# First masked attention: the mask's matmuls open every other step and close the rest, and two queues bring the operand stacks

## The chip, the cores and the metric

The kernel is one program on 1 core of a Trainium2 chip. The metric is the device time in microseconds of one execution. Every duration below comes from one profiled execution, or from the repeated timings, which are named as such.

## What is computed

Four examples of 512 rows and 256 features pass through a masked cross attention, a routed mixture of eight experts, a second cross attention with memory rows and a quantized feed-forward stack. Only the first attention is touched:

```python
def L0_xattn(q, kv, mask):              # q = layernorm(x), kv = ctx, 16 heads of 16
    qh, kh, vh = heads(q @ Wq.T + bq), heads(kv @ Wk.T + bk), heads(kv @ Wv.T + bv)
    attn = einsum('bhqd,bhkd->bhqk', qh, kh) * 16 ** -0.5
    attn = softmax(where(mask, -inf, attn), axis=-1)     # one mask for all heads
    return concat_heads(einsum('bhqk,bhkd->bhqd', attn, vh)) @ Wo.T + bo

x = x + L0_xattn(layernorm(x), ctx, mask)      # the part that the change touches
x = x + L0_ffn(layernorm(x))                   # 8 experts, one per row, gated
x = x + L1_xattn(layernorm(x), ctx)            # 16 heads of 64, 128 memory rows
x = x + L1_ffn(layernorm(x))                   # three residual quantized blocks
return x                                       # x: 4 x 512 x 256, float32
```

## The kernel before

`attention0` runs first, over the four examples. One pass over an example is a **turn**. The 16 heads go in four **groups** of four, g = 0 to 3, and each group in eight **steps**, j = 0 to 7. A step treats one tile of 128 keys (kt = j // 2) for one pair of heads (slot = j % 2), against all 512 queries. A prologue before the first turn does the same preparation that a turn does for the next example.

TensorE (PE) is the engine that does most of the work. Its order within a step is the table `STEPS` (lines 144 to 153), whose words stand for:

- `score` (L667): scores of one head, 64 rows by 128 columns of the array, 512 queries streamed. The two heads of a pair lie in the two halves of the rows and go together. `q_stack` and `k_stack` hold each head's 16 features three times, as rounded and remaining parts (hi, hi, lo against hi, lo, hi), with the negated row maximum in the last row.
- `bias` (L677): four 64 by 64 bf16 matmuls that add the mask to both heads' scores in PSUM. The last one tells ScalarE, through `s_full`, that the step's scores are whole.
- `maximum`, `early` (L639): scores in the other orientation, of the next group (`early`: the one after it), whose row maxima VectorE takes. Two such matmuls lie in the two halves of the rows. A group has 16: four early, twelve in steps 0 to 5.
- `times_v` (L687): exponentials times values, 128 rows by 32 columns a head, eight records for four heads. It follows the exponential of the step before its own, which ScalarE reports in `exp_done`.
- `query`, `key` (L619): projections for the next half of the heads, in g = 0 and 2. `turn` (L646) transposes the group's maxima; `sums` (L651) spreads the previous group's reciprocal sums; `rows` (L605) transposes normalized rows.

The matmuls of `maximum`, `turn`, `sums`, `query` and `key` share three PSUM banks, `p_m`, in rotation. `Banks.free` makes PE wait until the bank taken three fills earlier has been read. The scores have two buffers, `p_s`; a step waits in `score` until the exponential two steps back is done.

VectorE (DVE) follows PE's fills in the same order: `maximum` (L468) adds the mask, reduces and frees the bank. It also splits projections (`split`, L460: lo = full - hi), normalizes (L485) and reads out the turn's last matmuls. ScalarE (ACT) writes `full` and `hi` (L353), takes the exponentials (L362) and copies outputs (L366).

The **stacks** are brought by DMA (`bring`, L252) from `hi` and `lo`, 64 KB a DMA, six for one stack and group. All are issued from SyncE's queue (SP), in this order for each half: queries' stack of the half's first group, keys' stack of that group, the maxima of group g + 1 (`bring_maxima`, L270), then both stacks of the half's last group. The reader of the first group's stacks is the `early` of step 6 in g = 0 and g = 2. GpSimd (POOL) takes reciprocal square roots (L320) and adds the output bias (L326), once an example.

## Time and profile before

| | |
|---|---|
| median of 3 runs | 1547.67 us (1545.13 to 1551.35) |
| the profiled execution, its own time | 1540.11 us |
| its span, first to last instruction | 1538.3 us |
| mean granted TensorE clock over the span | 0.936 of full speed |
| first attention: prologue, then four turns | 0 to 48 us, 48 to about 394 us |

The profile has a page (busy shares, 40 slices, queues, chains, groups of instructions) and views of the trace: a timeline of instructions in order of time, a list of waits, and busy times of chosen stretches. A record of a matmul begins with its weight load when that load is not hidden, and ends after the pipeline is through, so records of neighbouring matmuls overlap. What counts is the distance between starts. A releaser in brackets is what ended the idle time before an instruction. `PEld` is the weight load, and `SPq` an issue on SyncE's queue.

### The profile page before, as it was taken

The page shows a single profiled execution, that of the slowest core. Times are in us where ns is not written, and L with a number is a line of the kernel's source. Part 1 is how long each engine was busy: PE and PEld are TensorE (multiplying, and loading weights), DVE is VectorE, ACT ScalarE, POOL GpSimd, SP SyncE. Part 2 cuts the span into 40 slices and gives each one's busy share as a digit, 9 for nine tenths or more (in the row PEclk, how much of TensorE's full clock was granted, in tenths as well). Part 3 has the DMA queues.
Part 4 walks back from the last instruction along what each step waited for, and adds up shares of the span by engine and source line. Part 5 has one row for each costly group of instructions (what it writes and reads, how often), then busy time and mean ns, then how long its engine had stood idle before and what let it go on. Part 6 is the DMA issues. An engine that isn't in the chain of part 4 may idle for free. (4 is left out here: it accounts for less than half of the span.)

```text
span 1538.3 us, 19109 instructions
## 1 busy us (share of the span) xinstructions
PE 1377.1 (90%) x6106; PEld 733.4 (48%) x6106; DVE 876.9 (57%) x1738; ACT 477.4 (31%) x678; POOL 450.0 (29%) x262
## 2 busy tenths in 40 slices
PE   4889889989554999966999999999999999998997
PEld 2324333343352776642444455444544455435886
DVE  5656666555341222236576655756576665786677
ACT  1343434435111222211333332333233332341221
POOL 2000000000123000031454534445354543473443
PEclk8799999899756999986999999999999999999998
DMA  6410112101238988844556552655256552610001
GB/s 181 162 43 8 51 40 55 42 22 23 68 122 252 319 309 312 313 117 107 88 77 96 83 83 42 97 82 83 41 82 96 82 82 43 113 63 21 0 1 55
DMA packets 71273, 152.13 MB, mean 99 GB/s; under 512 B 17888, under 2 KB 28640, under 8 KB 64544
## 3 DMA queue, kind: packets, MB, share of 16 engines
q1 hardware_dynamic: 65392, 143.82, 41.2%
q0 software_dynamic: 2640, 7.21, 1.4%
q8 instruction: 37, 0.61, 0.2%
q10 hardware_dynamic: 3168, 0.20, 0.1%
q14 instruction: 36, 0.29, 0.1%
HBM read 75.49 MB, written 10.22 MB: 56 GB/s over the span
## 5 line engine op out<-in xcount | busy, mean ns | idle before, releaser
L1198 POOL TENSOR_TENSOR a_probs<-a_probs 128x1024 f32<-128x1024 f32 x128 | 304.9, 2382 | 379.2 <-PE a_p_mo L1868 378.7
L1270 ACT ACTIVATE a_probs<-a_p_s 128x1024 f32<-128x1024 f32 x160 | 163.8, 1024 | 340.7 <-PE a_p_s L1854 340.7
L468 DVE CUSTOM_DVE_ANT_0 a_scratch<-a_p_m,a_bias_q 128x512 bf16<-128x512 f32 x256 | 163.3, 687 | 97.3 <-PE a_p_m L639 97.2
L1502 DVE TENSOR_REDUCE a_max_ctx<-a_p_mo 128x1 f32<-128x512 f32 x256 | 161.5, 684 | 75.1 <-PE a_p_mo L1825 75.1
L362 ACT ACTIVATE a_probs<-a_p_s 128x1024 f32<-128x1024 f32 x128 | 129.1, 1024 | 113.6 <-PE a_p_s L677 112.3
L1868 PE MATMUL a_p_mo<-a_probs,a_v 128*64 128x512 f32 x512 | 139.0, 621 | 0.0
L1853 PE MATMUL a_p_s<-a_q_hh,a_k_hl 128*128 128x512 f32 x256 | 128.5, 502 | 0.0
L639 PE MATMUL a_p_m<-a_k_stack,a_q_stack 63*128 63x512 f32 x256 | 88.9, 543 | 24.3 <-DMA a_k_stack<-a_hi 22.1
L1525 DVE RECIPROCAL a_recip<-a_p_mo 128x512 f32<-128x512 f32 x32 | 107.4, 3355 | 5.0 <-PE a_p_mo L1877 4.9
L1854 PE MATMUL a_p_s<-a_q_lm,a_k_h 65*128 65x512 f32 x256 | 101.9, 398 | 0.0
L1246 ACT ACTIVATE a_o_norm<-a_p_mo,a_b 128x128 f32<-128x128 f32 x184 | 49.9, 382 | 151.9 <-PE a_p_mo L1730 151.9
L1720 PE MATMUL a_p_s<-a_w,a_o_raw 128*128 128x512 f32 x184 | 84.7, 604 | 0.0
L1740 PE MATMUL a_p_mo<-a_w,a_o_norm 128*128 128x256 f32 x368 | 83.3, 379 | 0.1
L1853 PEld LDWEIGHTS a_p_s<-a_q_hh,a_k_hl 128*128 128x128 f32 x256 | 49.1, 192 | 63.3 <-issue 37.2
L1825 PE MATMUL a_p_mo<-a_k_hl,a_q_hh 64*128 64x512 f32 x256 | 67.6, 484 | 11.6 <-DMA a_q_lm<-a_lo 7.5
L687 PE MATMUL a_p_o<-a_probs,a_v 128*32 128x512 f32 x512 | 71.7, 633 | 6.8 <-ACT a_probs L362 4.8
L1419 DVE COPY a_o_norm<-a_p_s 128x512 f32<-128x512 f32 x46 | 31.8, 692 | 74.7 <-PE a_p_s L1720 74.7
L1493 DVE SCALAR_TENSOR_TENSOR a_lo<-a_p_mo,a_bqk,a_hi 128x512 fp32r<-128x512 f32 x58 | 43.2, 745 | 54.6 <-ACT a_hi L1260 52.1
L1740 PEld LDWEIGHTS a_p_mo<-a_w,a_o_norm 128*128 128x128 f32 x368 | 68.2, 190 | 9.1 <-issue 0.8
L1260 ACT ACTIVATE a_hi<-a_p_mo,a_bqk 128x512 fp32r<-128x512 f32 x58 | 39.9, 687 | 100.5 <-PE a_p_mo L1799 100.5
L320 POOL TENSOR_TENSOR a_rstd<-a_rstd,a_minus_half 128x4 f32<-128x4 f32 x4 | 4.1, 1024 | 225.9 <-DVE a_rstd L428 225.9
L1799 PE MATMUL a_p_mo<-a_xn_t,a_space 128*128 128x512 f32 x116 | 62.6, 666 | 6.9 <-DVE a_recip L1525 6.5
(221 smaller groups left out, 2110.3 us busy)
## 6 DMA issues: line engine op xcount, KB each, us to landing
a_w<-in_L_w SPq DMA_DIRECT2D x46, 1024.0 KB, 6.6
a_q_hh<-a_hi SPq DMA_DIRECT2D x64, 256.0 KB, 5.1
a_k_hl<-a_hi SPq DMA_DIRECT2D x64, 128.0 KB, 6.1
a_k_hl<-a_lo SPq DMA_DIRECT2D x64, 128.0 KB, 6.5
a_k_h<-a_hi SPq DMA_DIRECT2D x32, 256.0 KB, 7.8
a_q_lm<-a_lo SPq DMA_DIRECT2D x32, 256.0 KB, 6.8
a_ctx_t<-in_ctx_t SPq DMA_DIRECT2D x8, 512.0 KB, 4.3
a_q_stack<-a_hi SPq DMA_DIRECT2D x64, 64.0 KB, 2.2
```

What stands on the lines that cost most here:

```text
L362: act.activation(probs[:, j % 4, :, :], p_s[:, j % 2, :, :], ACT.Exp).then_inc(exp_done.sem, 1)
L468: dve.tensor_tensor_reduce(scratch[:, fill.n % M_BANKS, :], m, bias_q[:, t, :], 1.0, -3.0e38, ALU.add, ALU.max, mx[:, g % 2, at:at + 1]).t ...
L639: done(pe.matmul(m, q_stack[rows, pair, P * t:P * (t + 1)], k_stack[rows, pair, :], start=True, stop=True))
L1198: pool.tensor_tensor(probs[:, kt], probs[:, kt - 1], probs[:, kt], ALU.add)\
L1270: act.activation(probs[:, kt, :, :], p_s[:, (KT1 * p + kt) % 2, :, :], ACT.Exp).then_inc(exp_done.sem, 1)
L1502: dve.tensor_reduce(max_ctx[:, NT * head + t:NT * head + t + 1], m, AX, ALU.max)\
L1525: dve.reciprocal(recip[:], m).then_inc(m_free.sem, 1)
L1720: mm = pe.matmul(p_h[:, HALVES * (n % 2) + half, :], rows_t[:, n % 2, k, :], w1[:, n % RING, k, S * half:S * (half + 1)], start=(k == 0), ...
L1740: mm = pe.matmul(p_y, hidden[:, n % 2, d, :], w2[:, n % RING, d, :], start=(d == 0), stop=(d == FC - 1))
L1853: pe.matmul(p_s[:, n % 2, i, :], first, q_hh[:, s, :], start=True, stop=False)
L1854: mm = pe.matmul(p_s[:, n % 2, i, :], second, q_lm[:, s, :], start=False, stop=True)
L1868: mm = pe.matmul(p_o[DK * i:DK * (i + 1), :], vh, probs[:, kt, i, :], start=(kt == 0), stop=(kt == KT1 - 1))
```

## The change

Even steps 2, 4 and 6 keep scores first and have the mask's matmuls end the accumulation; odd steps 1, 3 and 5 and step 0 begin with the mask's, and the second score ends it and signals `s_full`. In steps 2 and 4 the two maxima now stand between scores and mask, and in step 7 the scores and two early maxima do. `sums` moves from the head of step 7 to step 6, between `turn` and the first two early maxima. The keys' stacks are issued from GpSimd's queue, both groups of a half in one go, with semaphores of their own. In the prologue, VectorE's three small operations for `nan_row` come after the early maxima, and the DMA that makes `bias_s` follows `bias_k` directly.

```diff
-        SCORE2 = ("score", "score", "bias")
-        STEPS = (("query", *SCORE2, *MAX2, "times_v"),
-                 ("key", *SCORE2, *MAX2),
-                 (*SCORE2, *MAX2, "times_v"),
-                 (*SCORE2, *MAX2),
-                 (*SCORE2, *MAX2, "times_v"),
-                 (*SCORE2, *MAX2),
-                 (*SCORE2, "times_v", "turn", *EARLY2),
-                 ("sums", *SCORE2, *EARLY2, "rows"))
+        SCORE2 = ("score", "score")
+
+        STEPS = (("query", "bias", *SCORE2, *MAX2, "times_v"),
+                 ("key", "bias", *SCORE2, *MAX2),
+                 (*SCORE2, *MAX2, "bias", "times_v"),
+                 ("bias", *SCORE2, *MAX2),
+                 (*SCORE2, *MAX2, "bias", "times_v"),
+                 ("bias", *SCORE2, *MAX2),
+                 (*SCORE2, "bias", "times_v", "turn", "sums", *EARLY2),
+                 (*SCORE2, *EARLY2, "bias", "rows"))
...
-        stacked = [Count(sem("stacked_first"), 16 * 24), Count(sem("stacked_last"), 16 * 24)]
+        stacked = [Count(sem(f"{stack}_{group}"), 16 * 12) for stack in ("queries", "keys") for group in ("first", "last")]
...
+        def bring(queue, half, group, n):
...
+                    queue.dma_start(stack[HALF * side + DH0 * k:HALF * side + DH0 * (k + 1), at:at + G0 // 2, :].bitcast(F32),
+                                    part[src:src + SLOT, n, :].bitcast(F32)).then_inc(stacked[2 * n + group].sem, 16)
...
             def stack(b, half):
 
-                for n in range(2):
-                    split_ready.wait(sp, b, 2 * half + n + 1)
-                    bring(half, 0, n)
+                split_ready.wait(sp, b, 2 * half + 1)
+                bring(sp, half, 0, 0)
 
             def stack_last(half):
 
-                for n in range(2):
-                    bring(half, 1, n)
+                bring(sp, half, 1, 0)
...
+            def stack_keys(b, half):
+                split_ready.wait_apart(pool, b, 2 * half + 2, consts, 2)
+                for group in range(2):
+                    bring(pool, half, group, 1)
+
             invert_deviation(-1)
+            stack_keys(-1, 2)
             pool.wait_ge(loaded, 16 * 5)
             bias(-1)
             with pool.Fori(0, B - 1) as b:
+                stack_keys(b, 1)
                 invert_deviation(b)
                 bias(b)
+                stack_keys(b, 2)
+            stack_keys(B - 1, 1)
...
-            dve.tensor_scalar(bias_k[:], mask_in[:, 1, :, :], -MASKED, None, ALU.mult)
+            dve.tensor_scalar(bias_k[:], mask_in[:, 1, :, :], -MASKED, None, ALU.mult).then_inc(prep, 1)
             dve.wait_ge(prep, 2)
-            dve.tensor_reduce(least_masked[:], bias_q[:], AX, ALU.max).then_inc(prep, 1)
...
             for i in range(N_MAX):
                 maximum(-1, fill, NG0, i)
             turn_maxima(-1, fill, NG0)
             for i in range(N_EARLY):
                 maximum(-1, fill, NG0 + 1, i)
+            dve.tensor_reduce(least_masked[:], bias_q[:], AX, ALU.max).then_inc(prep, 1)
...
+            def free_scores(b, g, j):
+
+                n = PARTS * g + j
+                if n >= 2:
+                    exp_done.wait_apart(pe, b, n - 1, consts, 2)
...
-                pe.matmul(p_s[:, slot, i, :], k_stack[rows, pair, P * kt:P * (kt + 1)], q_stack[rows, pair, :],
-                          start=True, stop=False)
+                mm = pe.matmul(p_s[:, slot, i, :], k_stack[rows, pair, P * kt:P * (kt + 1)], q_stack[rows, pair, :],
+                               start=not masked, stop=masked)
+                if masked and i == 1:
+                    mm.then_inc(s_full.sem, 1)
...
-                        mm = pe.matmul(p_s[keys, slot, i, :], ident_b[rows, rows], bias[rows, kt, :], start=False, stop=True)
-                mm.then_inc(s_full.sem, 1)
+                        mm = pe.matmul(p_s[keys, slot, i, :], ident_b[rows, rows], bias[rows, kt, :], start=not scored, stop=scored)
+                if scored:
+                    mm.then_inc(s_full.sem, 1)
```

On PE, steps 4 and 5 of group 1 in a turn. `a_p_s<-a_q_stack` is the pair of scores, `a_p_s<-a_bias` the mask, `a_p_m<-a_k_stack` a maximum, `a_p_o` the values product. Before:

```order
L667 MATMUL a_p_s<-a_q_stack,a_k_stack 128x512 x2
L677 MATMUL a_p_s<-a_bias_k,a_ident_b 64x512 x2
L677 MATMUL a_p_s<-a_bias_s,a_ident_b 64x512 x2
L62 REGISTER_ALU
L639 MATMUL a_p_m<-a_k_stack,a_q_stack 128x512
L62 REGISTER_ALU
L639 MATMUL a_p_m<-a_k_stack,a_q_stack 128x512
L62 REGISTER_ALU
L687 MATMUL a_p_o<-a_probs,a_v 32x512 x4
L667 MATMUL a_p_s<-a_q_stack,a_k_stack 128x512 x2
L677 MATMUL a_p_s<-a_bias_k,a_ident_b 64x512 x2
L677 MATMUL a_p_s<-a_bias_s,a_ident_b 64x512 x2
```

Now:

```order
L679 MATMUL a_p_s<-a_q_stack,a_k_stack 128x512 x2
L62 REGISTER_ALU
L648 MATMUL a_p_m<-a_k_stack,a_q_stack 128x512
L62 REGISTER_ALU
L648 MATMUL a_p_m<-a_k_stack,a_q_stack 128x512
L691 MATMUL a_p_s<-a_bias_k,a_ident_b 64x512 x2
L691 MATMUL a_p_s<-a_bias_s,a_ident_b 64x512 x2
L62 REGISTER_ALU
L702 MATMUL a_p_o<-a_probs,a_v 32x512 x4
L691 MATMUL a_p_s<-a_bias_k,a_ident_b 64x512 x2
L691 MATMUL a_p_s<-a_bias_s,a_ident_b 64x512 x2
L679 MATMUL a_p_s<-a_q_stack,a_k_stack 128x512 x2
```

The two maxima stand ahead of the mask now, and the next step's mask follows the values product. Scores and maxima of an odd step and the even step after it are now neighbours.

On PE, steps 6 and 7 of group 1; `a_ident,a_mx` is `turn`, `a_recip_rows,a_spread` is `sums`. Before:

```order
L687 MATMUL a_p_o<-a_probs,a_v 32x512 x4
L62 REGISTER_ALU x2
L646 MATMUL a_p_m<-a_ident,a_mx 16x128
L62 REGISTER_ALU
L639 MATMUL a_p_m<-a_k_stack,a_q_stack 128x512 x2
L62 ISA
L651 MATMUL a_p_m<-a_recip_rows,a_spread 128x512
L667 MATMUL a_p_s<-a_q_stack,a_k_stack 128x512 x2
L677 MATMUL a_p_s<-a_bias_k,a_ident_b 64x512 x2
L677 MATMUL a_p_s<-a_bias_s,a_ident_b 64x512 x2
L62 REGISTER_ALU
L639 MATMUL a_p_m<-a_k_stack,a_q_stack 128x512
```

Now:

```order
L702 MATMUL a_p_o<-a_probs,a_v 32x512 x4
L62 REGISTER_ALU x2
L655 MATMUL a_p_m<-a_ident,a_mx 16x128
L62 REGISTER_ALU
L62 ISA
L660 MATMUL a_p_m<-a_recip_rows,a_spread 128x512
L648 MATMUL a_p_m<-a_k_stack,a_q_stack 128x512 x2
L679 MATMUL a_p_s<-a_q_stack,a_k_stack 128x512 x2
L648 MATMUL a_p_m<-a_k_stack,a_q_stack 128x512
L62 REGISTER_ALU
L648 MATMUL a_p_m<-a_k_stack,a_q_stack 128x512
L691 MATMUL a_p_s<-a_bias_k,a_ident_b 64x512 x2
```

`sums` stands ahead of the first two early maxima, and step 7's scores have early maxima, then the mask, behind them.

On POOL, from the head of the loop over examples. Before:

```order
L332 ISA
L320 TENSOR_TENSOR a_rstd<-a_rstd,a_minus_half 128x4
L62 REGISTER_ALU
L326 ISA
L326 TENSOR_TENSOR x_all<-x_all,a_bo 128x1024
L332 REGISTER_ALU
L332 COMPARE_AND_BRANCH
```

Now:

```order
L337 ISA
L237 DMA a_k_stack<-a_hi 16x2x512 x2
L237 DMA a_k_stack<-a_lo 16x2x512 x2
L237 DMA a_k_stack<-a_hi 16x2x512 x4
L237 DMA a_k_stack<-a_lo 16x2x512 x2
L237 DMA a_k_stack<-a_hi 16x2x512 x2
L62 ISA
L319 TENSOR_TENSOR a_rstd<-a_rstd,a_minus_half 128x4
L62 REGISTER_ALU
L325 ISA
L325 TENSOR_TENSOR x_all<-x_all,a_bo 128x1024
L68 REGISTER_ALU
```

Twelve issues precede the reciprocal square root, and twelve more follow the bias. SP keeps the queries' issues and the maxima between them.

## Rows read from the trace of the kernel before

**Rows 1.** Busy times of one turn: us, then PE, PEld, DVE, ACT, POOL busy, granted clock, DMA.

```profile
141.38:233.05 91.67, 82.55 (x469) 33.23 (x468) 57.95 (x167) 39.22 (x44) 3.39 (x2) 0.98 0.17 41
```

**Rows 2.** Waits of PE, 48 to 400 us: who, on whom, us, times, longest.

```profile
PE a_p_m L639 <- DMA a_k_stack<-a_hi: 15.6, 7, 2.6
```

**Rows 3.** Timeline (start us, us), 204.8 to 208.5 us, steps 1 and 2 of group 3.

```profile
204.85 0.50 PE L667 MATMUL a_p_s<-a_q_stack,a_k_stack 64*128 64x512 f32 x2
...
205.28 0.11 PEld L677 LDWEIGHTS a_p_s<-a_bias_k,a_ident_b 64*64 64x64 bf16 x2 [0.25 <-issue]
...
205.62 0.50 PE L639 MATMUL a_p_m<-a_k_stack,a_q_stack 63*128 63x512 f32 x2
...
205.95 0.40 PE L667 MATMUL a_p_s<-a_q_stack,a_k_stack 64*128 64x512 f32 x2
...
206.28 0.11 PEld L677 LDWEIGHTS a_p_s<-a_bias_k,a_ident_b 64*64 64x64 bf16 x2 [0.37 <-issue]
...
207.01 0.18 PEld L639 LDWEIGHTS a_p_m<-a_k_stack,a_q_stack 63*128 63x128 f32 x1 [0.21 <-DVE a_mx L468]
...
207.44 1.07 PE L687 MATMUL a_p_o<-a_probs,a_v 128*32 128x512 f32 x8
...
208.44 0.49 PE L667 MATMUL a_p_s<-a_q_stack,a_k_stack 64*128 64x512 f32 x2
```

**Rows 4.** Timeline, 144 to 165 us, group 0 of example 1: keys' stacks and their reader.

```profile
144.83 1.98 PE L619 MATMUL a_p_m<-a_ctx_t,a_wk 128*128 128x512 f32 x4 [0.36 <-ACT a_hi L353]
...
151.21 0.69 DVE L460 TENSOR_TENSOR a_lo<-a_full,a_hi 128x512 fp32r<-128x512 f32 x1
...
153.98 1.19 SPq L252 DMA_DIRECT2D a_k_stack<-a_hi  x2
...
156.96 0.28 PE L646 MATMUL a_p_m<-a_ident,a_mx 128*16 128x128 f32 x1
...
159.40 0.50 PE L639 MATMUL a_p_m<-a_k_stack,a_q_stack 63*128 63x512 f32 x2 [2.16 <-DMA a_k_stack<-a_hi]
```

**Rows 5.** Timeline, 466 to 500 us, DMAs that GpSimd issues.

```profile
467.18 0.96 POOL L1173 DMA_INDIRECT x_slots<-a_probs,a_slot  x1 [0.30 <-issue]
...
496.68 0.60 POOL L1179 DMA_DIRECT2D y_slots<-a_yb  x1 [15.19 <-DVE a_yb L1426]
```

**Rows 6.** DMA issues: KB each, median us from issue to landing.

```profile
a_k_stack<-a_hi SPq DMA_DIRECT2D x64, 64.0 KB, 2.2
...
y_slots<-a_yb POOLq DMA_DIRECT2D x23, 128.0 KB, 2.6
```

**Rows 7.** Busy times, from a first early maximum to the second values product behind it.

```profile
251.05:258.68 7.63, 6.96 (x43) 2.85 (x43) 6.81 (x24) 4.20 (x5) 1.02 (x1) 1.00 0.44 104
291.13:302.85 11.72, 11.72 (x44) 3.73 (x45) 5.80 (x16) 4.36 (x5) 0.00 (x0) 0.56 0.28 68
```

**Rows 8.** Timeline, 20 to 50 us, the prologue.

```profile
21.58 0.69 DVE L460 TENSOR_TENSOR a_lo<-a_full,a_hi 128x512 fp32r<-128x512 f32 x1 [0.94 <-ACT a_hi L353]
...
26.25 2.28 DVE L561 TENSOR_REDUCE a_least_masked<-a_bias_q 128x4 f32<-128x2048 bf16 x1
...
30.19 1.19 PE L639 MATMUL a_p_m<-a_k_stack,a_q_stack 63*128 63x512 f32 x3 [6.50 <-DMA a_k_stack<-a_hi]
...
49.78 0.69 DVE L468 CUSTOM_DVE_ANT_0 a_scratch<-a_p_m,a_bias_q 128x512 bf16<-128x512 f32 x1 [4.86 <-PE a_p_m L639]
```

**Rows 9.** Timeline, 214.6 to 221 us, the end of group 3, example 1.

```profile
215.00 0.28 PE L646 MATMUL a_p_m<-a_ident,a_mx 128*16 128x128 f32 x1
...
215.81 1.12 PE L651 MATMUL a_p_m<-a_recip_rows,a_spread 128*128 128x512 f32 x2
...
217.08 0.68 DVE L485 TENSOR_TENSOR a_o_norm<-a_o_norm,a_p_m 128x512 f32<-128x512 f32 x1
217.29 0.11 PEld L677 LDWEIGHTS a_p_s<-a_bias_k,a_ident_b 64*64 64x64 bf16 x2 [0.24 <-issue]
...
218.83 1.06 PE L687 MATMUL a_p_o<-a_probs,a_v 128*32 128x512 f32 x8 [0.70 <-ACT a_probs L362]
```

More of the change, by code:

```diff
@@ L226, in bank @@
                 return p_m[:, (BEFORE + self.n - 1) % M_BANKS, :]
+        halves = ((q_stack, (hi, hi, lo)), (k_stack, (hi, lo, hi)))
+        def bring(queue, half, group, n):
+            stack, parts = halves[n]
+            at = PAIR0 // 2 * (half % 2) + G0 // 2 * group
+            for k, part in enumerate(parts):
+                for side in range(2):
+                    src = HALF * group + SLOT * side
+                    queue.dma_start(stack[HALF * side + DH0 * k:HALF * side + DH0 * (k + 1), at:at + G0 // 2, :].bitcast(F32),
+                                    part[src:src + SLOT, n, :].bitcast(F32)).then_inc(stacked[2 * n + group].sem, 16)
         @block.sync
@@ L349, in project @@
                 for count in stacked:
-                    count.wait(act, b, 16 * 12 * half)
+                    count.wait(act, b, 16 * 6 * half)
                 at = half % 2
@@ L458, in split @@
                     for count in stacked:
-                        count.wait(dve, b, 16 * 12 * half)
+                        count.wait(dve, b, 16 * 6 * half)
                 dve.tensor_tensor(lo[:, n, :], full[:, n, :], hi[:, n, :].bitcast(F32),
@@ L464, in maximum @@
                 m = fill.bank()
-                m_full.wait_apart(dve, b, fill.n, prep, 5)
+                m_full.wait_apart(dve, b, fill.n, prep, 3)
                 side, t, pair = maximum_of(i)
@@ L637, in maximum @@
                 if i == 0:
-                    stacked[g % 2].wait(pe, b, 16 * 12 * (g // 2 + 1))
+                    for n in range(2):
+                        stacked[2 * n + g % 2].wait(pe, b, 16 * 6 * (g // 2 + 1))
                 done(pe.matmul(m, q_stack[rows, pair, P * t:P * (t + 1)], k_stack[rows, pair, :],
@@ L698, in turn @@
                     for j in range(PARTS):
-                        head = 0
+                        head, masked = 0, False
                         for what in steps(g, j, ahead):
+                            if what in ("score", "bias") and not head and not masked:
+                                free_scores(b, g, j)
                             if what in ("query", "key"):
```

31 lines of the change are left out of this document (10 added, 21 removed).

## Prediction

> **What bounds the kernel now.** I read four views in this order. The busy times of one turn come first [rows 1]: in 91.67 us PE is busy 82.55, DVE 57.95, ACT 39.22 and POOL 3.39. PE bounds this stage, so what a part is worth is read from its path. The list of waits shows where PE stands still [rows 2]: 15.6 us in seven waits of up to 2.6 us for a keys' stack. The timeline of two ordinary steps shows what PE's order costs [rows 3]. The timeline of group 0 shows how the seven waits arise [rows 4]. The prologue [rows 8] and the end of a turn [rows 9] complete the picture. Behind 394 us no code that runs is changed, and I cost that part at nothing.
>
> The steps in [rows 3] are to be read by their starts. The scores start at 204.85, their mask at 205.28, the maxima at 205.62, the next scores at 205.95, their mask at 206.28, the fourth maximum at 207.01, the values product at 207.44, and the following step at 208.44. A pair of steps thus takes 3.59 us. Scores behind another tile shape need 0.43 to the mask, and scores behind maxima, which have their shape, need 0.33: the weight load is hidden, worth 0.10. The first maximum to the fourth takes 1.39 us. There are three banks, so the fourth waits until DVE has read the first. This small loop, not the matmuls, sets part of each pair.
>
> **The change, part by part. Pairs of steps (1,2) and (3,4).** After the change a pair is mask (0.34), scores (0.33), first maximum, fourth maximum, mask, values product. First to fourth is again DVE's round trip, 1.39 less 0.10, because the first maximum's weight load is hidden behind the scores: 1.29. From the fourth maximum to another shape takes 0.43, the mask 0.34, the values product 1.00. The sum is 3.73 against 3.59, so **a pair gets 0.14 us longer** although it changes the array's shape twice less. The saved 0.10s go into the wait for the bank, and the last mask now stands behind that wait instead of in front of it. In groups 1 and 3 this is on the path. In groups 0 and 2 it lies beside the wait for the stack. Steps 5 and 6 stay equal within 0.05: the values product of step 6 waits for step 5's exponential before and after.
>
> The Trainium skill (TensorEngine Tiling (Array Packing), Key Properties) says that changing the tiling mode drains TensorE. The 0.10 agrees with that. By the rule alone, some ten fewer changes in each of 16 groups, at 0.10, would give back 16 us; by the sum of rows the bank's wait keeps most of it.
>
> **Keys' stacks.** In [rows 4] the keys' projection starts at 144.83 and DVE begins the second split at 151.21, done near 151.8. SP is still issuing queries' stacks, so the keys' six issues run from 153.98 at 0.6 us each; the last lands 2.2 later [rows 6], and the maximum starts at 159.40, 14.57 behind the projection, after 2.16 of idleness. PE has been ready since about 157.2. From POOL the keys' first issue can start at about 151.9. No row shows POOL issuing plain DMAs back to back. The nearest ones bound the distance: SP's 0.6 below, and GpSimd's indirect DMAs above, 0.96 and 0.30 between two, 1.26 [rows 5]. I take a plain one's duration, 0.54 to 0.60 (first shown), with that gap of 0.30: **0.845 us**. For the landing I take 2.2; 2.6 is the median of the plain ones on POOL's queue, twice as large and among heavier traffic [rows 6]. The last of six then lands 5 x 0.845 + 2.2 = 6.4 behind 151.9, at 158.3. Bounds: 5 x 0.6 + 2.2 = 5.2 and 5 x 1.26 + 2.6 = 8.9, at 157.1 and 160.8. With the first maxima of a turn 0.1 earlier, as step 1 is shorter up to them, the early maximum comes 13.4 behind the projection instead of 14.57.
>
> The page DMA: Bandwidth & Descriptors of the Trainium skill (Issuing engines are not separate DMA queues) holds that several issuers save only the sequencer's time, usually small beside the transfer. Here a row disagrees with "small": six issues take 3.7 us against 2.2 to a landing.
>
> **Groups 0 and 2.** Group 0 gains 1.15 at its early maximum. Behind it the order scores, two maxima, mask, then mask, scores, maxima, values product makes the values product wait for step 7's exponential: 1.39 + 0.43 + 1.54 = 3.36 from the early maximum, against 3.0 before (2.8 by the distances of [rows 3], 3.04 in example 2). The 1.54 runs from a mask over its exponential to the product behind it, 217.29 to 218.83 in [rows 9]. Net -0.8. In group 2 `sums` (0.2 for `turn` and 1.05 for itself) moves into the wait, where it costs nothing; its cover is the stack. PE reaches the early maximum near 13.5, at the stack's arrival: -1.05. Behind it 3.5 stand against 4.1 before: -0.5. Net -1.55.
>
> **Groups 1 and 3.** Group 1 pays two pairs, +0.3, and wins 0.2 in step 0, where two masks meet; its end hangs on DVE's copies in both orders. I take 0. Group 3 pays 0.3 in pairs. At its end, `turn` starts at 215.00 and the last product at 218.83, 3.83 later [rows 9]. Now `sums` starts at +0.2, the early maximum at +1.25, DVE has normalized at +2.1 (215.81 to 217.08 plus 0.6, taken from `sums`) and frees the first early bank 0.75 later, the fourth maximum follows at +2.85, the mask at +3.3, the product at +4.85: +1.0. Net +1.2, with 0.05 of steps 5 and 6 back.
>
> **A turn:** -0.8 + 0 - 1.55 + 1.2 = -1.15, three times -3.5. The last turn has one such stack: -0.8, pairs in groups 1 and 2 and the longer way from `turn` of group 1 to the next product, +0.5 in the sum.
>
> **Prologue.** The second split ends near 22.2 and the first maximum starts at 30.19 [rows 8]. POOL's issues give 22.25 + 4.2 + 2.2 = 28.7: -1.5. DVE is ready then, since its 2.28 us reduction and two operations of 0.17 move behind the early maxima. They fit into the 4.86 us that DVE idles ahead of 49.78; without that cover they would cost 2.6. POOL's bias addition moves back by ten issues or so; it is read at the end of the turn, some 90 us later. The square root of the loop starts near 164.7, and POOL's twelve issues from 151.9 end at 162.0, free by 2.7 us. The shorter wait of SP costs nothing.
>
> **Clock.** In five of seven cases the granted clock falls from full (2.4 GHz) to half (1.2 GHz) behind the long wait. From the early maximum to the second product behind it takes 7.63 at a clock of 1.00 and 11.72 at 0.56 [rows 7], the most of five such stretches; their excess is 8.4 us together (1.5, 1.5, 0.3, 4.0, 1.1). What PE did ahead of each was 2 to 2.6 us of nothing. With 1 us or none left I take back 6 of the 8.4.
>
> **Sum:** -3.5 + 0.5 - 1.5 - 6 = -10.5 us. The profiled execution took 1540.1 in its own time, 1.8 more than its span and 7.6 under the median of the runs; I subtract from the median: 1547.7 - 10.5 = **1537 us**.
>
> **The rivals.**
> - *The clock stays as it is* (0.22). New waits for the fourth maximum, about 0.8 us a pair, stand where none was, so a fall may come anyway. For it: two of seven long waits were followed by no fall, so length alone does not decide. Without the 6 the change gives -4.5: 1543.
> - *POOL issues slowly* (0.16), the one that ends **slower**. At 1.26 us a DMA the keys' stack comes 2.1 later than I forecast, seven times, 14.7; the prologue loses 2.1 and the clock's 6 do not come back: -10.5 + 22.8 = +12, 1560. It decides from 0.96 us between issues on: each 0.1 is worth 4 us, and without the clock only 4.5 are at stake. For it: the only back-to-back DMAs on POOL have 1.26. Against: a plain one lasts 0.54 to 0.60, not 0.96.
> - *POOL issues as fast as SP* (0.13). At 0.6 PE finds the stack landed: group 0 gains 0.9 more four times, the prologue 1.2, the clock the other 2.4: 1530.
> - *Changes of shape are the bound* (0.03): -26, 1521. Against: the bank's wait in [rows 3].
> - *The stacks are not brought sooner* (0.04), because both queues share the same DMA engines. Groups 0 and 2 then keep their arrival, +1.15 four times and +1.05 three times, and prologue and clock give nothing: +5, 1552. Against: the DMA share of the turn is 0.17 [rows 1]. This is what the Trainium skill's page on DMA would make of it.
>
> **How the numbers follow.** The forecast has 0.42, with its own range from 1532 to 1541. About 0.5%, 7.7 us, is what a measurement of this kernel can tell from no change. The range 1528 to 1558 takes in the forecast, the clock's rival, the fast queue and most of the slow one. Faster by over 0.5%: 0.36 of the forecast's 0.42, the fast queue and the shape rival, and a little of the clock's, 0.53. Slower: 0.14 of the slow queue and a little more, 0.15. The rest, 0.32, lies within.
>
> **What would show it.** Issues of keys' DMAs on POOL 0.8 to 0.9 apart; the wait for `a_k_stack` down from 15.6 to about 4 us; pairs at 3.7 in groups 1 and 3, with first to fourth maximum at 1.3; a last product 4.8 behind `turn`; the first maximum near 28.7; a first attention at full clock behind the stacks. I would be wrong if the issues are over 0.96 apart, if the half-clock stretches remain, or if pairs fall under 3.5.

## The result, and the profile after

| | kernel before | changed kernel |
|---|---|---|
| median of the runs made side by side | 1547.67 us | 1540.05 us |
| the same in a second session | 1550.41 us | 1535.11 us |
| ratio, first and second session (95%) | | 0.9928 [0.9903, 0.9954], 0.9917 [0.9885, 0.9949] |
| profiled execution, its span, mean granted clock | 1540.11, 1538.3, 0.936 | 1534.38, 1532.6, 0.938 |
| mean of the runs with a recorded clock, mean clock | 1548.8 ±1.0 (55), 0.9310 | 1537.3 ±2.0 (14), 0.9357 |

One of the nine runs behind the median of 1540.05 us fell in a slow state (2232.55 us at a clock of 0.633), and the ratios and means leave it out.

By the means of its runs the change makes the kernel 10.6 us faster in the first session and 12.7 in the second (0.7 to 0.8%), 11.5 together. The forecast had 10.5. The terms of the sum fared less well than the sum. For the second session I had expected 1536 to 1543 us, a ratio of 0.990 to 0.996, and half clock for 17 to 27 us of the stretch from 50 to 400 us. The median of 1535.11 is just under, the ratio is met, and the half clock is not: it stood for some 35 us, worked out from the stretch's mean clock of 0.95.

The list of PE's waits between 48 and 400 us answers to [rows 2] (who, on whom, us in total, times, longest):

```profile
PE a_p_o L702 <- ACT a_probs L370: 13.1, 29, 1.1
PE a_p_m L648 <- DVE a_mx L476: 12.5, 29, 0.5
...
PE a_p_m L648 <- DMA a_k_stack<-a_hi: 3.5, 5, 1.0
```

The wait for the keys' stack fell from 15.6 us to 3.5. Two waits that were small, or not among the first, stand above it now: 29 waits for a bank of the maxima, and 29 for an exponential, which had 4.8 us in 7 waits before. Both are the new order's own.

The timeline of group 0 of example 1 answers to [rows 4] (start us, us, engine, line, operation; in brackets idle time and what ended it):

```profile
140.74 1.98 PE L627 MATMUL a_p_m<-a_ctx_t,a_wk 128*128 128x512 f32 x4 [0.65 <-ACT a_hi L361]
...
146.93 0.69 DVE L468 TENSOR_TENSOR a_lo<-a_full,a_hi 128x512 fp32r<-128x512 f32 x1
...
148.21 1.00 POOL L237 DMA_DIRECT2D a_k_stack<-a_hi  x2 [44.73 <-DVE a_lo L468]
...
149.20 1.00 POOL L237 DMA_DIRECT2D a_k_stack<-a_lo  x2
...
150.20 2.00 POOL L237 DMA_DIRECT2D a_k_stack<-a_hi  x4
...
154.14 0.50 PE L648 MATMUL a_p_m<-a_k_stack,a_q_stack 63*128 63x512 f32 x2 [0.78 <-DMA a_k_stack<-a_hi]
```

The early maximum stands 13.40 us behind the keys' projection, as forecast (13.4; 14.57 before). Hardly a step on the way there is as forecast. The second split is done at 147.62. GpSimd's first issue starts 0.59 later, where I had 0.1; SyncE starts 0.03 behind its own split. The issues follow each other at 0.50 us, where I had 0.845, so the sixth starts at 150.70. From there 3.44 pass until the maximum, where I had 2.2 to the landing. The DMA issues answer to [rows 6] (KB each, median us to landing):

```profile
a_q_stack<-a_hi SPq DMA_DIRECT2D x64, 64.0 KB, 2.2
a_k_stack<-a_hi POOLq DMA_DIRECT2D x64, 64.0 KB, 3.2
```

The busy times show what the transfers meet. The first row is of the kernel before, the second of the changed one (us, busy time of PE, PEld, DVE, ACT and POOL, granted clock, DMA share, GB/s):

```profile
150.00:163.00 13.00, 10.72 (x73) 3.77 (x73) 8.89 (x29) 6.00 (x7) 0.00 (x0) 0.94 0.37 90
```

```profile
150.00:156.00 6.00, 4.48 (x37) 1.73 (x37) 2.98 (x12) 2.30 (x3) 4.19 (x9) 1.00 0.77 147
```

GpSimd's second group of six goes out at once behind the first, beside SyncE's. The DMA engines' share doubles: from the first group's first issue to its maximum it is 0.79 now (148.21 to 154.14) and was 0.39 before (153.98 to 159.40). How much of the longer landing comes of that is tested below.

A pair of steps in group 3 answers to [rows 3]:

```profile
197.69 0.50 PE L679 MATMUL a_p_s<-a_q_stack,a_k_stack 64*128 64x512 f32 x2
198.03 0.40 PE L648 MATMUL a_p_m<-a_k_stack,a_q_stack 63*128 63x512 f32 x2
...
199.33 0.50 PE L648 MATMUL a_p_m<-a_k_stack,a_q_stack 63*128 63x512 f32 x1 [0.42 <-DVE a_mx L476]
199.76 0.40 PE L691 MATMUL a_p_s<-a_bias_k,a_ident_b 64*64 64x512 bf16 x2
...
200.10 1.07 PE L702 MATMUL a_p_o<-a_probs,a_v 128*32 128x512 f32 x8
...
201.44 0.50 PE L679 MATMUL a_p_s<-a_q_stack,a_k_stack 64*128 64x512 f32 x2
```

From scores to scores it takes 3.75 us (forecast 3.73, before 3.59), and from the first to the fourth maximum 1.30 (forecast 1.29, before 1.39). The fourth waits 0.42 for a bank.

The end of group 3, here of example 0, answers to [rows 9]:

```profile
118.50 0.28 PE L655 MATMUL a_p_m<-a_ident,a_mx 128*16 128x128 f32 x1
...
118.62 1.02 PE L660 MATMUL a_p_m<-a_recip_rows,a_spread 128*128 128x512 f32 x2
...
119.57 0.49 PE L648 MATMUL a_p_m<-a_k_stack,a_q_stack 63*128 63x512 f32 x2
...
119.68 0.69 DVE L493 TENSOR_TENSOR a_o_norm<-a_o_norm,a_p_m 128x512 f32<-128x512 f32 x1 [0.49 <-PE a_p_m L660]
...
122.99 1.06 PE L702 MATMUL a_p_o<-a_probs,a_v 128*32 128x512 f32 x8 [1.13 <-ACT a_probs L370]
```

The last product is 4.49 behind `turn`, forecast 4.85, before 3.83. I had expected VectorE to be done normalizing at +2.1; it is done at +1.87, and the fourth maximum, forecast at +2.85, starts at +2.53.

The prologue answers to [rows 8]:

```profile
20.89 0.69 DVE L468 TENSOR_TENSOR a_lo<-a_full,a_hi 128x512 fp32r<-128x512 f32 x1 [1.40 <-ACT a_hi L361]
21.50 1.22 DVE L562 TENSOR_SCALAR a_bias_q<-a_mask_in 128x2048 bf16<-128x2048 uint8 x1
...
22.29 1.68 POOL L237 DMA_DIRECT2D a_k_stack<-a_hi  x2 [12.77 <-DVE a_lo L468]
...
23.96 1.79 POOL L237 DMA_DIRECT2D a_k_stack<-a_lo  x2
24.43 1.22 DVE L567 TENSOR_SCALAR a_bias_k<-a_mask_in 128x2048 bf16<-128x2048 uint8 x1
25.74 2.00 POOL L237 DMA_DIRECT2D a_k_stack<-a_hi  x4
...
30.67 1.19 PE L648 MATMUL a_p_m<-a_k_stack,a_q_stack 63*128 63x512 f32 x3 [7.67 <-DMA a_k_stack<-a_hi]
```

The first maximum is at 30.67, forecast 28.7, before 30.19. The split ends 0.7 sooner than before (21.58 against 22.27), so from its end the way has become longer by 1.2. The first pair of GpSimd's issues holds one of 1146 ns, the second one of 1292, where 507 is usual. Both long ones lie beside a conversion of the masks on VectorE. The sixth issue starts at 26.24.

What a turn gained is read by pieces that lie at full clock in both traces, from the query projection over the four `turn` products (T0 in group 0 to T3 in group 3) to the next query projection:

| piece | before | changed | difference |
|---|---|---|---|
| query to T0 | 233.05 to 248.61: 15.56 | 137.22 to 153.09: 15.87 | +0.31 |
| T0 to T1 | 248.61 to 266.45: 17.84 | 244.22 to 261.04: 16.82 | -1.02 |
| T1 to T2 | 266.45 to 288.76: 22.31 | 169.84 to 191.82: 21.98 | -0.33 |
| T2 to T3 | 197.39 to 215.00: 17.61 | 191.82 to 207.79: 15.97 | -1.64 |
| T3 to query | 215.00 to 233.05: 18.05 | 118.50 to 137.22: 18.72 | +0.67 |

The sum is -2.0 us a turn, where the forecast had -1.15.

**Clock against work.** All runs but those of the kernel before in the first session are recorded with their mean granted clock. Within one and the same kernel, a run with a mean clock higher by 0.001 is 1.21 us shorter (±0.12, over these 155 runs, with a mean of its own for each kernel). With it each kernel's mean is carried over to one clock, 0.936. That is an estimate of mine, and it parts what a kernel gains in work and waits from what it gains in clock. The ± are 1.96 standard errors, somewhat narrow for six runs:

| kernel (runs) | mean us | mean clock | at clock 0.936 |
|---|---|---|---|
| before (55) | 1548.8 ±1.0 | 0.9310 | 1542.8 ±0.8 |
| changed (14) | 1537.3 ±2.0 | 0.9357 | 1536.9 ±1.1 |
| e2_order (12) | 1547.7 ±1.6 | 0.9303 | 1540.8 ±1.4 |
| e1_queues (12) | 1542.5 ±3.2 | 0.9337 | 1539.7 ±1.3 |
| g1_no_prologue (12) | 1539.1 ±2.4 | 0.9351 | 1538.0 ±1.2 |
| e3_sums (10) | 1537.0 ±2.6 | 0.9369 | 1538.1 ±1.3 |
| keys apart (e4 and f2, 12) | 1531.5 ±2.6 | 0.9397 | 1536.0 ±1.3 |
| f4_split_maxima (6) | 1532.0 ±5.1 | 0.9367 | 1532.8 ±1.7 |
| g4_wait_back (6) | 1564.7 ±4.0 | 0.9253 | 1551.8 ±2.1 |

By this estimate the change is worth 5.9 us at equal clock and 0.0047 of clock, 5.7 us.

**Where the clock is lost.** The traces show the stretches at half clock themselves. Two places matter in the four turns: a fall within 3 us of one of the seven maxima that read a new keys' stack, and the way from the `turn` product of group 3 to the next query projection. In us at half clock:

| trace | behind the seven stacks | at the three ends of a turn |
|---|---|---|
| before | 30.6 | 0 |
| changed, first and second trace | 3.4, 6.8 | 10.2, 10.2 |
| e1_queues | 10.2 | 0 |
| e2_order | 27.2 | 3.4 |
| g4_wait_back | 37.4 | 10.2 |

Each row is of single traces, which vary from run to run. Even so, most of the half clock behind the stacks is gone, as forecast, and g4_wait_back, which brings the wait back, brings it back. At the turn's end, where the kernel before has none, a part of it has come back: eleven of the twelve traces with the new order have some there (in the changed kernel's second one, from 216.9 to 223.7 us), and neither of the two with the old order. The values product there waits 1.13 us for the exponential instead of 0.70; whether that wait is the cause is not shown.

### The profile page after: what moved, and what is told of

It is laid out like the page before. It is cut to its first block and busy times, and to the rows that moved or that the text cites. A ratio compares the mean times of both kernels' runs of the same rounds, so it can differ in the third digit from the quotient of the medians.

```text
span 1532.6 us, 19262 instructions
## 1 busy us (share of the span) xinstructions
PE 1364.1 (89%) x6106; PEld 734.7 (48%) x6106; DVE 879.5 (57%) x1738; ACT 477.2 (31%) x678; POOL 500.0 (33%) x358
## 5 line engine op out<-in xcount | busy, mean ns | idle before, releaser
L237 POOL DMA_DIRECT2D a_k_stack<-a_hi x64 | 32.9, 520 | 234.7 <-DVE a_lo L468 234.6
L648 PE MATMUL a_p_m<-a_k_stack,a_q_stack 63*128 63x512 f32 x256 | 83.5, 463 | 28.9 <-DVE a_mx L476 13.4
L702 PE MATMUL a_p_o<-a_probs,a_v 128*32 128x512 f32 x512 | 69.5, 615 | 13.1 <-ACT a_probs L370 13.1
L1197 POOL DMA_DIRECT2D y_slots<-a_yb x23 | 12.6, 546 | 175.3 <-DVE a_yb L1444 175.3
```

The lines of the kernel that those rows point to most:

```text
L648: done(pe.matmul(m, q_stack[rows, pair, P * t:P * (t + 1)], k_stack[rows, pair, :], start=True, stop=True))
```

## The experiments

My theory at the start was that of the forecast: the keys' stacks come sooner because GpSimd issues them, and the fewer stalls give clock back. The rivals: the order of the steps does it, or the clock was luck. In the experiments "equal clock" is the last column of the table above, an estimate.

### The two halves apart: e1_queues and e2_order

e1_queues is the kernel before with the keys' stacks from GpSimd, and nothing else of the change:

```diff
+            def stack_keys(b, half):
+                split_ready.wait_apart(pool, b, 2 * half + 2, consts, 2)
+                for group in range(2):
+                    bring(pool, half, group, 1)
```

> The kernel before with the keys' stacks issued from GpSimd and nothing else of the change. Theory: the gain is the stacks'. The wait of the early maxima behind turn falls from 2.4 to about 1.3 us in all seven cases (-8), half-clock time falls with it (-5), pairs stay at 3.59 and the first maximum stays near 30.7: 1534 to 1537, at least as fast as the whole change. Rival, the order brings the gain: the waits fall but the time stays within 3 us of before, 1545 to 1549.

e2_order is the kernel before with the new STEPS and PE's functions for them; SyncE brings all stacks.

> The kernel before with the new order of steps and the mask opening or ending the sums, all stacks from SyncE. Theory: pairs at 3.73, last product 4.85 behind turn, stack's wait still about 2.4 from turn to early maximum but with the sums inside it; +1 us a turn, 1548 to 1552 unless the clock helps. Rival, fewer changes of the array's shape are the gain: 1538 or less, pairs under 3.5.

Measured: e1_queues 1544.26 us, 0.9956 [0.9930, 0.9983]; e2_order 1547.31 us, 0.9991 [0.9971, 1.0012]. The waits of PE, first of e1_queues, then of e2_order:

```profile
PE a_p_m L647 <- DMA a_k_stack<-a_hi: 8.9, 7, 1.7
```

```profile
PE a_p_o L694 <- ACT a_probs L363: 12.7, 27, 1.1
PE a_p_m L640 <- DVE a_mx L469: 12.6, 28, 1.0
PE a_p_m L640 <- DMA a_k_stack<-a_hi: 11.3, 7, 2.7
```

The queue alone takes 6.7 us out of the wait for the stacks and gives 3.1 us at equal clock, and most likely some clock, though the two means overlap (0.9337 ±0.0025 against 0.9310 ±0.0007). The order alone brings the two waits of 12.6 and 12.7 us, as in the changed kernel, and hides a part of the wait for the stacks behind `sums`. It gives 2.0 us at equal clock, hardly more than the uncertainty of the two means (1.4 and 0.8), and no clock. The order by itself isn't the source of the gain. Of what I expected, e1_queues missed: 1544.26 lies above 1534 to 1537, since the early maxima come 1.2 to 2.0 behind `turn` (1.3 expected); by the means the queue alone is 5 us slower than the whole change, where I had it at least as fast. e2_order came in just under its 1548 to 1552, with the last product 4.50 behind `turn` instead of 4.85.

### Without the prologue's edit: g1_no_prologue

```diff
+            dve.tensor_reduce(least_masked[:], bias_q[:], AX, ALU.max).then_inc(prep, 1)
...
             for i in range(N_MAX):
                 maximum(-1, fill, NG0, i)
             turn_maxima(-1, fill, NG0)
             for i in range(N_EARLY):
                 maximum(-1, fill, NG0 + 1, i)
-            dve.tensor_reduce(least_masked[:], bias_q[:], AX, ALU.max).then_inc(prep, 1)
```

> The change without its edit of the prologue: VectorE prepares the NaN row before the first maxima, as in the kernel before; queues and order of the steps are the changed ones. The queues alone measured 0.9956 of the kernel before and the order alone 0.9991; the whole change 0.9917 and 0.9928. If the parts add, this is at 0.9947 (1541 us) and the prologue's edit is worth the missing 4 us, which would be three times what was forecast for it. If queues and order need one another, and the prologue's edit is worth 1.5 us or less as forecast, it is at 0.9925 to 0.9935 (1538 to 1539 us).

Measured: 1538.64 us, 0.9939 [0.9915, 0.9964]. At equal clock it is 4.8 us under the kernel before; e1 and e2 have 3.1 and 2.0, so within the uncertainty these parts add. The clock, 0.9351, is that of the changed kernel within its interval. The ratio, 0.9939, lies between the two that I had expected (0.9947 if the parts add, 0.9925 to 0.9935 if they need one another), and its interval holds both. The prologue's edit is left with 1.1 us at equal clock, which is within the uncertainty; the traces are sharper. From the first maximum to the first query projection of the loop pass 15.15 us in e1 and 15.34 here, and 14.18 in the changed kernel. So the edit is worth 1.0 to 1.2 us where GpSimd brings the keys; with SyncE (kernel before, e2) 14.18 was had without it. The rows of g1_no_prologue show why:

```profile
29.93 4.25 DVE L571 TENSOR_SCALAR a_nan_row<-a_least_masked 128x4 f32<-128x4 f32 x1
...
31.77 2.36 POOL L325 TENSOR_TENSOR x_all<-x_all,a_bo 128x1024 f32<-128x1024 f32 x1
```

One of VectorE's three small operations takes 4.25 us (4.27 in e1_queues), where it takes 0.17 in the kernel before, in e2_order and in the changed kernel. It ends 0.05 us behind GpSimd's bias addition, which the issues of the keys' stacks have pushed back from 14.57 us to this place, and VectorE's first maximum waits for it. Whether the issues or the bias addition held it is not separated. The forecast let the bias addition move back at no cost; that holds only because the small operations moved away too.

### VectorE keeps GpSimd from issuing: f3_masks_act

```diff
-            dve.tensor_scalar(bias_q[:], mask_in[:, 0, :, :], -MASKED, None, ALU.mult).then_inc(prep, 1)
...
-            dve.tensor_scalar(bias_k[:], mask_in[:, 1, :, :], -MASKED, None, ALU.mult).then_inc(prep, 1)
...
+            for n, dst in enumerate((bias_q, bias_k)):
+                act.activation(dst[:], mask_in[:, n, :, :], ACT.Copy, scale=-MASKED).then_inc(prep, 1)
```

> The changed kernel with the prologue's two conversions of the masks to bf16 done by ScalarE instead of VectorE. Theory that VectorE keeps GpSimd from issuing while it converts: all 12 issues of the prologue take 500 to 530 ns (two took 1146 and 1292 in the changed kernel), the keys' first stack lands 1 to 1.4 us sooner and the first maximum is at 29.3 to 29.8 us instead of 30.67. Rival, the two long issues come from a full descriptor ring or from the transfers of the weights: two of the issues stay above 1000 ns and the first maximum at 30.5 or later. Either way the total moves by 1.5 us at most.

Measured: 1536.95 us, 0.9912 [0.9877, 0.9946]. Its prologue:

```profile
22.73 1.91 ACT L419 ACTIVATE a_bias_q<-a_mask_in 128x2048 bf16<-128x2048 uint8 x1
...
24.27 1.30 POOL L237 DMA_DIRECT2D a_k_stack<-a_hi  x2 [13.40 <-DVE a_lo L471]
24.53 1.91 ACT L419 ACTIVATE a_bias_k<-a_mask_in 128x2048 bf16<-128x2048 uint8 x1
...
25.56 1.00 POOL L237 DMA_DIRECT2D a_k_stack<-a_lo  x2
26.55 1.99 POOL L237 DMA_DIRECT2D a_k_stack<-a_hi  x4
...
31.43 1.19 PE L649 MATMUL a_p_m<-a_k_stack,a_q_stack 63*128 63x512 f32 x3 [6.43 <-DMA a_k_stack<-a_hi]
```

With the conversions on ScalarE the second long issue is gone and the first has shrunk from 1146 to 758 ns. What is left of the first is not explained. The first maximum follows the first issue after 7.16 us instead of 8.38 (8.34 in the second trace of the changed kernel). That is the 1.2 us of the theory. The absolute 29.3 to 29.8 wasn't reached, since this execution's query projection began 1.4 us later, and "all at 500 to 530" missed by the one of 758. By its time, 31.43, the first maximum would fit the rival's "30.5 or later"; but the rival's two issues above 1000 ns are gone, and the distance from the first issue is what it left out. The Trainium skill (SBUF — State Buffer, in the section SBUF: two separate sides) says that VectorE in certain SBUF-to-SBUF modes locks GpSimd out of the port pair that the two share, so that it can't write the descriptors of its DMAs. The rows agree: 1146 and 1292 beside the conversions, 507 elsewhere. I had costed the prologue without looking at what VectorE does beside the issues. In the total nothing is to be seen of it.

### What the second group costs the first: e4_keys_apart and f2_keys_apart_again

```diff
                 for group in range(2):
+                    if group:
+                        stacked[2].wait_apart(pool, b, 16 * 6 * (half + 1), consts, 2)
                     bring(pool, half, group, 1)
```

> The whole change, but GpSimd issues the keys of a half's second group only when those of the first have landed. Theory: the twelve issues 0.5 us apart beside SyncE's six crowd the DMA engines, so landings take 3.2 instead of 2.2; with six in flight the first group's last lands 0.5 to 1 us sooner, early maximum 0.2 to 0.5 sooner (turn plus sums bounds it at 1.05 behind turn where there are sums), first maximum near 29.5: -2 to -4 us, 1536 to 1539. Rival, landings from GpSimd are slow by themselves: no difference, first maximum at 30.7.

> The changed kernel with GpSimd holding back the keys' second stack until their first has landed, again. Crowding theory: fewer of the transfers share the DMA engines, each group's stacks land by the time they are due, and this kernel stays 6 to 10 us under the changed kernel of the same call (the first measurement had 8). Clock theory: the attention takes the same time in both (last products at 398.5 and 399.6 us so far) and the difference lay in the half-clock windows behind it, so the two are within 3 us of each other here. In both, the early maxima of even groups come 1.0 to 1.1 us after the maxima's transpose, bound by the sums.

Measured: e4 1530.33 us, 0.9884 [0.9854, 0.9915]; f2, the same kernel in another session, 1533.96 us, 0.9887 [0.9854, 0.9920], beside the changed kernel's 0.9917 [0.9885, 0.9949]. The wait for the stacks and the busy times of the crowded stretch, in f2:

```profile
PE a_p_m L650 <- DMA a_k_stack<-a_hi: 2.5, 4, 1.0
```

```profile
152.50:158.50 6.00, 4.79 (x41) 1.82 (x37) 3.28 (x12) 2.33 (x3) 2.93 (x7) 1.00 0.45 93
```

This trace runs 2.5 us later in the group, so its stretch is taken 2.5 us later: the engines' share is 0.45 instead of 0.77, and the wait 2.5 us instead of 3.5. In group 0 the early maximum comes 0.70 to 1.29 behind `turn` in these two traces, in the changed kernel's first 0.98 to 1.30. But the median landing stays at 3.0 to 3.1 us, so the second group explains only a part of the slower landing. Issue by issue, the sixth of a first group lands after 3.0 us (median of eight in each trace), where the changed kernel has 3.4 and 3.5 and the kernel before 2.2: holding the second group back returns some 0.4 of 1.2, where I had expected 0.5 to 1. SyncE's transfers still run partly beside the first group, the issues stand closer, and the queue is another one; which of these costs the rest is not shown. In the prologue nothing is won: the first maximum comes 8.4 and 8.2 us behind the first issue, as in the changed kernel (8.4 and 8.3), and the 29.5 us expected was 31.92 and 30.79. The kernels' means differ by 5.8 us, of which 0.9 at equal clock; the rest is clock, 0.9397 ±0.0020 against 0.9357 ±0.0013. The last matmul of the attention starts at 399.6 us in e4's trace and 401.1 in f2's (changed kernel 398.5 and 405.8, kernel before 411.5). Why the clock is higher isn't settled; the 6 to 10 us that the crowding theory expected in f2's session were not confirmed (1.2 by the medians, 4.1 by the means). e4's 1536 to 1539 was missed on the fast side.

### `sums` in its old place: e3_sums

```diff
-                 (*SCORE2, "bias", "times_v", "turn", "sums", *EARLY2),
-                 (*SCORE2, *EARLY2, "bias", "rows"))
+                 (*SCORE2, "bias", "times_v", "turn", *EARLY2),
+                 ("sums", *SCORE2, *EARLY2, "bias", "rows"))
```

> The whole change with the sums back at the head of step 7. Theory: in group 2 the sums no longer fill the wait, +1 in three turns; in groups 1 and 3 the early maxima come 1.05 sooner and the bank loop lies beside the sums, -0.5 each. Within 2 us of the whole change. Rival: the sums' place carries the gain of the change, 1545 or more.

Measured: 1536.72 us, 0.9923 [0.9900, 0.9947]; within 0.1% of the changed kernel of the first session. The early maximum of odd groups comes 0.21 behind `turn` instead of 1.07; but T2 to T3 takes 16.50 us (194.71 to 211.21) instead of 15.97, and T3 to the query 18.39 (to 229.60) instead of 18.72, so what is saved in one place is paid in the other. Where `sums` stands makes no difference that can be measured.

### The banks of the maxima: f4_split_maxima

```diff
-                 (*SCORE2, *MAX2, "bias", "times_v"),
-                 ("bias", *SCORE2, *MAX2),
+                 (*SCORE2, "maximum", "bias", "times_v"),
+                 ("bias", "maximum", *SCORE2, *MAX2),
```

(in steps 2 to 5)

> The changed kernel with one of the four maxima of each pair (steps 2 to 5) brought after the odd step's masks, so that the three banks aren't asked for four times in a row. If the pair is bound by the banks of the maxima (3.74 us, first to fourth maximum 1.30), a pair of steps takes 3.50 to 3.60 us with the wait of 4th maximum gone, the 6 undisturbed pairs of each two groups give 1 to 1.4 us, a turn 2 to 3 us and the kernel 6 to 10 us. Rival, the exponentials bound the pair (3.5 us of ScalarE): the pair stays at 3.65 to 3.75 with more waiting at the P.V products, and the kernel is within 3 us of the changed one.

Measured: 1533.50 us, 0.9878 [0.9843, 0.9913]. A pair of group 3, and the waits of PE:

```profile
204.62 0.40 PE L691 MATMUL a_p_s<-a_bias_k,a_ident_b 64*64 64x512 bf16 x2
...
206.36 0.50 PE L648 MATMUL a_p_m<-a_k_stack,a_q_stack 63*128 63x512 f32 x1 [0.19 <-DVE a_mx L476]
...
208.13 0.40 PE L691 MATMUL a_p_s<-a_bias_k,a_ident_b 64*64 64x512 bf16 x2
```

```profile
PE a_p_o L702 <- ACT a_probs L370: 16.9, 35, 1.1
PE a_p_m L648 <- DVE a_mx L476: 6.3, 21, 0.5
```

The pair is down from 3.75 to 3.51 us, in the range of the banks' theory. The waits for a bank are halved (12.5 to 6.3), but those for the exponential rise from 13.1 to 16.9: that is what comes next. A group of the same kind takes 15.74 us (195.57 to 211.31) instead of 15.97, half of what two pairs promised. The total is 4.1 us better at equal clock, under the 6 to 10 expected; beside the changed kernel of the same session, 1535.11, the intervals overlap.

### The wait put back: g4_wait_back

```diff
                         stacked[2 * n + g % 2].wait(pe, b, 16 * 6 * (g // 2 + 1))
+                    if g % 2 == 0:
+                        stacked[3].wait(pe, b, 16 * 6 * (g // 2 + 1))
```

> The changed kernel with the wait put back: TensorE's first early maximum of every even group waits until the keys' second stack has landed as well, some 3 us behind the transpose instead of 1.0 to 1.5 (2.4 to 2.8 in the kernel before). No work is added. Theory that such stalls cost clock too: over the runs the mean granted clock falls from 0.9355 to 0.931 or below, and the time rises by 5 to 7 us of waiting and another 4 to 6 us of clock, to 1546 to 1550 us. Rival, the clock has nothing to do with this wait: it stays within 0.001 of 0.9355, and the time rises by 5 to 7 us to 1542 to 1544 us.

Measured: 1566.14 us, 1.0115 [1.0077, 1.0152], 27 us above the changed kernel's mean. Its wait for the stacks from 48 us on, and the busy times of 50 to 400 us, of g4_wait_back, the changed kernel and the kernel before, in this order:

```profile
PE a_p_m L650 <- DMA a_k_stack<-a_hi: 19.5, 7, 3.3
```

```profile
50.00:400.00 350.00, 297.58 (x1707) 122.21 (x1710) 210.62 (x609) 145.40 (x163) 52.16 (x90) 0.92 0.20 48
```

```profile
50.00:400.00 350.00, 302.02 (x1807) 127.09 (x1807) 212.16 (x606) 152.71 (x171) 52.27 (x90) 0.97 0.18 42
```

```profile
50.00:400.00 350.00, 312.96 (x1775) 120.00 (x1774) 208.34 (x601) 152.92 (x170) 10.18 (x6) 0.95 0.16 42
```

The edit adds no matmul and no transfer. It adds 16.0 us of waiting in the seven even groups (19.5 - 3.5) and some 6 in the prologue (from the query projection to the loop's first one it takes 37.10 us instead of 30.45 and 31.23; the first maximum is at 37.67), 22 together. At equal clock that costs 14.9 us, and the mean clock falls from 0.9357 ±0.0013 to 0.9253 ±0.0032, another 12.6. The half clock behind the stacks is back too, 37.4 us of it. So the theory that such stalls cost clock holds, and "the clock has nothing to do with this wait" falls. My 5 to 7 us for the waiting was wrong: seven times 1.9 would have been 13 already, and I hadn't looked at the prologue, where this wait stands too.

### Putting the edits together: g2_split_apart and g3_split_apart_sums

> The changed kernel with both edits that gained on it: the keys' second stack held back, and one maximum of each pair of steps moved behind the odd step's masks. If the gains are of different waits they add: the two together at 1527 to 1531 us, 0.985 to 0.987 of the kernel before. If both had only met a better clock, it is at 1533 to 1537 us like the changed kernel.

> The same, with the sums' product back at the head of the last step. With the keys there in time, the first early maximum follows the transpose after 0.7 to 1.1 us and is held by the sums' bank in most groups (1.07 us). Theory that this bank is what is late next: the early maxima come 0.3 to 0.7 us after the transpose, each group gains up to 0.4 us and the kernel 3 to 5 us over the one with the sums in the seventh step. Rival, the wait moves to the last step's sums as in the kernel before (there 0.21 us and the sums later): within 2 us of it.

Measured: g2 (keys apart and split maxima) 1534.52 us, 0.9907 [0.9872, 0.9942]; g3 (`sums` back in step 7 as well) 1529.20 us, 0.9877 [0.9837, 0.9917]. g2 isn't better than either of its parts; what I expected of it, 1527 to 1531, was wrong. In g3 the early maxima of groups 0 and 2 come 0.42 to 1.26 behind `turn`. Its mean is 2.5 us under g2's, where 3 to 5 were expected. At equal clock g2, g3 and f4 stand at 1533.8, 1535.3 and 1532.8, each ±1.7 or 1.8: they can't be told apart. g3 had the lowest median of all (that of e4 is 1530.33), and e4 and g3 are both faster than the kernel before beyond doubt. That they are faster than the changed kernel is likely for e4 and f2 taken together (1531.5 ±2.6 against 1537.3 ±2.0) and open for g3.

## Why the prediction was right, point by point

- **The sum.** -10.5 forecast, -11.5 measured by the means, on the right side and near the forecast's time. By its terms: turns and last turn -3.0, prologue -1.5, clock -6. At equal clock -5.9 is measured where the first two give -4.5, and the clock is worth -5.7 by the estimate. That the sum is so near is partly luck: the three turns gained 2.5 us more than forecast (-6.0 for -3.5), and the prologue, forecast at -1.5, cost 1.2 to 2.0. The last turn's +0.5 can't be checked, as the kernel before has half clock in it.
- **Clock, -6: right in size, and in half of its path.** "With 1 us or none left I take back 6 of the 8.4": the runs' mean clock rose by 0.0047, worth 5.7 us, and g4_wait_back shows that such a wait is a cause. Behind the stacks the half clock went from 30.6 us to 3.4 and 6.8, as forecast. But "a first attention at full clock" did not come: 10.2 us of half clock stand at the ends of the turns, where there was none. The rival *the clock stays as it is* had this possibility in it, that a fall comes at a new wait. The agreement of 5.7 with 6 is partly luck, as this loss had no term. A single trace would not have shown the gain: the second trace of the changed kernel has 0.95 in the stretch from 50 to 400 us, as the kernel before has, the first has 0.97.
- **The keys' arrival, 13.4: right by errors that cancel.** "0.845 us" between issues is 0.50, outside even my lower bound of 0.6. "For the landing I take 2.2" is 3.2 by the median (3.4 for the sixth issue); my upper bound was 2.6. And the start of POOL behind the split, which I took as 0.1, is 0.59. Sooner by 1.7, later by 0.5 and 1.2: nothing is left of it. The rival *POOL issues as fast as SP* was right in its premise and wrong in its result, as it carried SyncE's landing time over to a stretch with twice the traffic. *The stacks are not brought sooner* failed; its reason, that all queues share the DMA engines, fits the landing's 1.2 us more, of which the test with the second group held back shows 0.4. The Trainium skill (DMA: Bandwidth & Descriptors, Issuing engines are not separate DMA queues) says that the DMAs of all issuing engines interleave on the same 16 DMA engines, and that several issuers save only the time to issue, "usually small relative to the DMA itself". The share of 0.79 for 0.39 agrees with the first; the "usually small" doesn't hold here, with six issues of 3.0 us together against 3.2 to a landing.
- **Pairs, +0.14: right.** 3.75 and 1.30 against 3.73 and 1.29; f4_split_maxima confirms the reason, the round trip of the three banks.
- **A turn, -1.15: too small, -2.0 measured.** By the pieces: group 0, from the query projection to T1, -0.71 (forecast -0.8); group 1, T1 to T2, -0.33 (forecast 0); T2 to T3, the rest of group 2 and group 3's pairs, -1.64 (forecast -1.55 + 0.3); group 3's end +0.67 (forecast +1.0). In T2 to T3 the early maximum is 1.17 sooner behind `turn` (2.37 to 1.20, forecast 1.05), and from it to the values product it takes 3.34 us, where I had 3.5 and before it was 4.09. At group 3's end the fourth maximum comes 0.3 sooner than costed. Why group 1 gained was not followed further.
- **Prologue, -1.5: wrong in sign.** "POOL's issues give 22.25 + 4.2 + 2.2" failed in the first and the last: the first issue starts 0.7 behind the split, and 4.4 pass from the start of the sixth to the maximum. The 4.2 is 3.95, since the two issues that VectorE stretches eat what the faster ones give. From the query projection to the loop's first one it takes 31.23 and 30.45 us in the two traces against 29.26, so +1.2 to +2.0. That VectorE's three small operations would be hidden was right; kept in their old place they would have cost 1.0 to 1.2 us (g1_no_prologue), not the 2.6 of the forecast.
- **The slow queue**, the rival with the other sign, was excluded by the first row of GpSimd's issues. Its price stood on the 1.26 us between indirect DMAs, which aren't plain ones.

## What to carry to other kernels

Moving issues to a second queue saved less here than the issuing time, because each landing took 1.2 us longer: put the landing time in the stretch after the move into the sum, not that of the stretch before. When a wait of TensorE is shortened, look at the granted clock over many runs as well as at the wait; here the clock was about half of the gain by my estimate, and the two traces of one and the same changed kernel differ in it by as much (0.95 and 0.97). Ask of a new order of work whether its own waits are followed by half clock too. Of a bank loop, ask how many fills stand in a row: spreading four over two steps gave back what keeping shapes together had cost.

## What the hardware did that I had not expected

- GpSimd issues plain DMAs back to back at 0.50 us, faster than SyncE's 0.6, but by the profile its first starts 0.59 us behind the split that it waits for (0.03 on SyncE), in every one of the seven cases in the turns.
- An issue on GpSimd that meets a 1.22 us conversion on VectorE takes 1146 or 1292 ns instead of 507.
- 22 us of waiting more, with no work added, take the mean granted clock from 0.9357 to 0.9253. Why it was 0.9397 with the second stack held back stays open.
- An operation of 0.17 us on VectorE takes 4.25 and 4.27 us when it meets GpSimd's issues and its bias addition, in g1_no_prologue and e1_queues.
